# Masked neighbour maximum: the second picks of two steps summed in one PSUM tile and taken once, colliding edges sent to the subset words, seven fetches for each block

## What is computed

```python
h = jnp.maximum(_layernorm(x, axis=-1), 0.0)
x = x + max_over_neighbours(h, adj)        # jnp.max(where(adj != 0, h, -inf)) for each node
h = jnp.maximum(_layernorm(x, axis=-1), 0.0)
hw = h @ W
e = (hw @ a1)[:, None] + (hw @ a2)[None, :]
e = jnp.where(e > 0, e, 0.2 * e)
e = jnp.where(adj > 0, e, -9e15)
x = x + jax.nn.elu(jax.nn.softmax(e, axis=1) @ hw)
```

## Time and profile before

| | |
|---|---|
| median of 3 timed runs | 742.74 us (741.84 to 743.23) |
| span of the profiled execution | 753.0 us |
| busy in it: PE, DVE, ACT, POOL | 681.6, 693.7, 473.1, 281.8 us |
| TensorE's mean granted clock | 0.990 of full speed |

### The profile page before, as it was taken

One profiled execution on the slowest core, in us unless ns is written; L12 is line 12 of the kernel. 1 busy time (PEld: TensorE's weight loads), 2 busy tenths in 40 slices (PEclk: granted clock), 3 DMA queues, 4 the chain that ended last, 5 costly groups with the idle time before them and its releaser, 6 DMA issues.

```text
span 753.0 us, 14749 instructions
## 1 busy us (share of the span) xinstructions
PE 681.6 (91%) x5560; PEld 490.6 (65%) x5560; DVE 693.7 (92%) x1023; ACT 473.1 (63%) x685; POOL 281.8 (37%) x259
## 2 busy tenths in 40 slices
PE   1788999999999999999999998699999999999994
PEld 1344655555555555555555554498998999999994
DVE  8999999999999999999999999988998999889893
ACT  3888999889898899998999897562433111001000
POOL 0612034434434535444444355441620294134040
PEclk9999999999999999999999999799999999999998
DMA  9999978997888888888888746342531544443400
GB/s 305 310 355 390 344 230 270 303 327 239 268 249 247 273 258 237 272 265 241 261 263 265 246 143 228 103 143 71 187 130 62 219 140 158 156 177 130 165 15 17
DMA packets 63000, 163.07 MB, mean 217 GB/s; under 512 B 6416, under 2 KB 11152, under 8 KB 58832
## 3 DMA queue, kind: packets, MB, share of 16 engines
q1 hardware_dynamic: 53776, 138.75, 54.2%
q0 software_dynamic: 9152, 23.34, 12.1%
HBM read 117.51 MB, written 44.56 MB: 215 GB/s over the span
## 4 chain that ended last, share of the span: by engine, by line
PE 53%; DVE 31%; issue 12%; ACT 2%; DMA 1%; DVEq 0%; another core or an unknown queue 0%; SPq 0%
PE pick_ps L714 23%; DVE acc L867 20%; PE pick_ps L613 17%; DVE rest L1054 5%; PE late_ps L627 4%; PE late_ps L585 4%; PE order_ps L594 2%; PE late_ps L693 1%; PE late_ps L623 1%; DMA best<-x 1%; DVE left L889 1%; ACT depth L403 1%; DVE found L915 1%; PE late_ps L714 1%; PE order_ps L680 1%
## 5 line engine op out<-in xcount | busy, mean ns | idle before, releaser
L867 DVE TENSOR_TENSOR acc<-pick_ps,acc 128x1024 f32<-128x1024 f32 x248 | 302.6, 1220 | 20.9 <-PE pick_ps L613 12.6
L363 POOL DMA_INDIRECT found<-subset_max,tops x192 | 204.4, 1065 | 271.8 <-DVE acc L867 187.5
L1054 DVE SCALAR_TENSOR_TENSOR rest<-depth,curves_sb,stage 128x512 f32<-128x512 f32 x256 | 199.5, 821 | 15.3 <-PE pick_ps L714 3.1
L714 PE MATMUL pick_ps<-keys,rest 128*128 128x129 f32 x1792 | 207.7, 276 | 3.3 <-DVE rest L1054 3.2
L714 PEld LDWEIGHTS pick_ps<-keys,rest 128*128 128x128 f32 x1792 | 204.6, 193 | 7.4 <-DVE rest L1054 5.8
L402 ACT ACTIVATE first<-order_ps 128x1024 f16<-128x1024 f32 x128 | 131.9, 1030 | 39.1 <-PE order_ps L594 33.0
L403 ACT ACTIVATE depth<-order_ps 128x1024 f16<-128x1024 f32 x128 | 131.5, 1027 | 0.0
L613 PE MATMUL pick_ps<-first,h_hi 128*128 128x512 f16 x256 | 97.3, 380 | 17.6 <-DVE acc L867 17.1
L613 PE MATMUL pick_ps<-second,h_hi 128*128 128x512 f16 x256 | 97.2, 380 | 15.2 <-DVE acc L867 14.7
L585 PEld LDWEIGHTS late_ps<-ident_h,stage 128*128 128x128 f16 x1024 | 68.4, 99 | 50.0 <-DMA stage<-adj 12.9
L613 PE MATMUL pick_ps<-first,h_lo 128*128 128x512 f16 x256 | 97.4, 380 | 0.0
(11 more groups left out here) (146 smaller groups left out, 599.9 us busy)
## 6 DMA issues: line engine op xcount, KB each, us to landing
stage<-adj SPq DMA_DIRECT2D x64, 1024.0 KB
edge_units<-edge_t SPq DMA_DIRECT2D x64, 512.0 KB
stage<-edge_units SPq DMA_DIRECT2D x32, 1024.0 KB, 4.8
subset_max<-keys POOLq DMA_DIRECT2D x13, 512.0 KB, 9.0
found<-subset_max,tops POOLq DMA_INDIRECT x192
best<-x SPq DMA_DIRECT2D x4, 512.0 KB, 5.9
subset_max<-x POOLq DMA_DIRECT2D x4, 512.0 KB, 6.6
out<-keys POOLq DMA_DIRECT2D x7, 256.0 KB, 2.8
```

What stands on the lines that cost most here:

```text
L363: nc.gpsimd.indirect_dma_start(found[:, n % NG, s, :], None, subset_max, bass.IndirectOffsetOnAxis(tops[:, n, s:s + 1], 0)).then_inc(gathe ...
L714: last = nc.tensor.matmul(out_ps(q, b), weight[:, n % WEIGHTS, b * P:(b + 1) * P], wh[:, c, :], start=c == 0 and starts(q, b), stop=c == C ...
L867: V.tensor_tensor(acc[:, q % 2, :], pick_ps[k][:, :], acc[:, q % 2, :], ALU.max).then_inc(raised, 1)
L1054: V.scalar_tensor_tensor(out=weight[:, n % WEIGHTS, :], in0=limit[:, q % 4, :], scalar=slope[:, c:c + 1], in1=units[:, m % EDGES, k * TI:( ...
```

## The change

For an even step g and the odd step g + 1, the two `pick(., 1)` now add into one PSUM tile (start at the even step, stop at the odd one), and VectorE takes the sum once, in the odd step. A sum of two is only right if no target has a second edge in both steps in the same half. So before ScalarE makes `depth` of an odd step, TensorE adds 0.5 to every rank of a target that had a second edge in the even step (`cross`: 2 matmuls of 512 columns, of a constant tile `cross_w` with `second` of the even step, into `order_ps`). Its depth then falls between the marks: the edge is no second edge there, and `rest` (its bound moved from 1.5 to 1.25, and steeper for the sigmoid) sends it to the words. There are then more words, and 7 rows are fetched in place of 6.

`second` is made for one step at a time (128 x 1024) in place of two (128 x 2048), right behind `take(g, 0)` and two steps ahead of its use. On ScalarE `select` is split: `firsts(g + 3)`, then `later`, then `depths(g + 3)`, which in odd steps waits for `crossed`. The fetches wait for `picked` in place of `raised`, whose count is now 3 for two steps.

```diff
-SHARP = 64.0
+SHARP = 128.0
 SLOTS = 8
-FETCHES = 6
+FETCHES = 7
...
+        cross_w = sb("cross_w", [P, P], F16)
...
+        def firsts_taken(g):
+            return 3 * (g // 2) + 1 + g % 2
+
+        def seconds_taken(g):
+            return 3 * (g // 2) + 3
+
+        def fetched(n, t):
+            return 16 * ((FETCHES + 1 - t % 2) // 2 * (n // NG) + t // 2 + 1)
...
-                            pool.wait_ge(raised, 2 * (STEPS + 2 + QUAD * n) + 4 + s)
+                            pool.wait_ge(picked, 2 * (STEPS + 2 + QUAD * n) + 4 + s)
...
-                def select(g):
+                def firsts(g):
                     act.wait_ge(ordered, g + 1)
                     if g >= 4:
                         act.wait_ge(picked, 2 * g - 7)
-                        act.wait_ge(second_ready, g // 2 - 1)
+                    nc.scalar.activation(first[:, g % 4, :], order_ps[:, :], ACT.Relu, scale=-1.0, bias=1.0 - MARK).then_inc(first_ready, 1)
+
+                def depths(g):
+                    if g % 2:
+                        act.wait_ge(crossed, g // 2 + 1)
+                    if g >= 4:
+                        act.wait_ge(second_ready, g - 3)
                         if (g // 2) % 2 == 0:
                             act.wait_ge(rest_even, g // 4)
                         else:
                             act.wait_ge(rest_odd, 2 * (g // 4) - 1 + g % 2)
-                    nc.scalar.activation(first[:, g % 4, :], order_ps[:, :], ACT.Relu, scale=-1.0, bias=1.0 - MARK).then_inc(first_ready, 1)
                     nc.scalar.activation(depth[:, g % 4, :], order_ps[:, :], ACT.Abs, bias=MARK - MID).then_inc(depth_ready, 1)
...
-                select(0)
+                firsts(0)
+                depths(0)
                 high(1)
                 edges(2)
-                select(1)
+                firsts(1)
                 edges(3)
-                select(2)
+                depths(1)
+                firsts(2)
+                depths(2)
...
-                        select(g + 3)
+                        firsts(g + 3)
                     if g % 4 == 0:
                         later(g + 2)
                     elif g % 4 == 2:
                         later(g + 1)
+                    if g + 3 < PAIRS:
+                        depths(g + 3)
...
+                def cross(g):
+                    pe.wait_ge(first_ready, g + 1)
+                    pe.wait_ge(second_ready, g)
+                    for c in range(PAIR):
+                        last = nc.tensor.matmul(order_ps[:, c * TI:(c + 1) * TI], cross_w[:, :], second[:, (g - 1) % 4, c * TI:(c + 1) * TI],
+                                                start=False, stop=True, skip_group_check=True)
+                    last.then_inc(crossed, 1)
...
-                        pe.wait_ge(second_ready, g // 2 + 1)
-                    if g >= 1:
-                        pe.wait_ge(raised, 2 * (g - 1) + k + 1)
+                        pe.wait_ge(second_ready, g + 1)
+                    if k == 0 and g >= 1:
+                        pe.wait_ge(raised, firsts_taken(g - 1))
+                    elif k == 1 and g >= 2 and g % 2 == 0:
+                        pe.wait_ge(raised, seconds_taken(g - 1))
                     s = first[:, g % 4, :] if k == 0 else second[:, g % 4, :]
                     for c in range(PAIR):
                         for part, half_h in enumerate((h_hi, h_lo)):
                             last = nc.tensor.matmul(pick_ps[k][:, c * TI:(c + 1) * TI], half_h[:, p * PAIR + c, :],
-                                                    s[:, c * TI:(c + 1) * TI], start=part == 0, stop=part == 1)
+                                                    s[:, c * TI:(c + 1) * TI], start=part == 0 and (k == 0 or g % 2 == 0), stop=part == 1 and (k == 0 or g % 2 == 1))
                     last.then_inc(picked, 1)
...
                flip(3)
+                cross(1)
                 rank(2)
...
+                    if g % 2 == 0 and g + 3 < PAIRS:
+                        cross(g + 3)
...
-                def seconds(m):
-                    at = 2 * m % 4
-                    dve.wait_ge(depth_ready, 2 * m + 2)
-                    if m >= 2:
-                        dve.wait_ge(picked, 4 * (m - 1))
-                    V.tensor_scalar(second[:, at:at + 2, :], depth[:, at:at + 2, :], MID - 1, None, ALU.is_equal).then_inc(second_ready, 1)
+                def seconds(g):
+                    dve.wait_ge(depth_ready, g + 1)
+                    if g >= 4:
+                        dve.wait_ge(picked, 2 * (g - 4) + 2)
+                    V.tensor_scalar(second[:, g % 4, :], depth[:, g % 4, :], MID - 1, None, ALU.is_equal).then_inc(second_ready, 1)
...
-                        V.tensor_tensor(found[:, at, 0:3, :], found[:, at, 0:3, :], found[:, at, 3:6, :], ALU.max).then_inc(halved, 1)
+                            for t in (FETCHES - 2, FETCHES - 1):
+                                dve.wait_ge(gathered[b % NG][t % 2], fetched(b, t))
+                        V.tensor_tensor(found[:, at, 0:3, :], found[:, at, 0:3, :], found[:, at, 4:7, :], ALU.max).then_inc(halved, 1)
...
-                        V.tensor_tensor(found[:, at, 0, :], found[:, at, 0, :], found[:, at, 1, :], ALU.max).then_inc(halved, 1)
+                        V.tensor_tensor(found[:, at, 0:2, :], found[:, at, 0:2, :], found[:, at, 2:4, :], ALU.max).then_inc(halved, 1)
...
                            V.tensor_tensor(h_lo[:, 0:QUARTER, :], hs[:, 0:QUARTER, :], h_hi[:, 0:QUARTER, :], ALU.subtract).then_inc(lo_first, 1)
+                            seconds(0)
...
+                V.memset(cross_w[:, :], 0.5)
...
-                seconds(0)
+                seconds(1)
                 for g in range(PAIRS):
                     q, p = g // STEPS, g % STEPS
                     take(g, 0)
+                    if g + 2 < PAIRS:
+                        seconds(g + 2)
                     if g % 4 == 0:
                         rests(g // 2)
-                    elif g % 2 and g + 1 < PAIRS:
-                        seconds(g // 2 + 1)
                     if g == PAIRS - 2:
                         scales(0)
                     if g == PAIRS - 1:
                         stat(1)
                         moments(1)
-                    take(g, 1)
+                    if g % 2:
+                        take(g, 1)
                     if g < len(CHAINS):
```

More of the change, by code:

```diff
@@ L410, in later @@
                         act.wait_ge(digested, 2 * (m - RESTS // 2 + 1))
-                    nc.scalar.activation(rest[:, to, :], depth[:, g % 4, :], ACT.Sigmoid, scale=-SHARP, bias=SHARP * (MID - 1.5)).then_inc(rest_odd, 1)
+                    nc.scalar.activation(rest[:, to, :], depth[:, g % 4, :], ACT.Sigmoid, scale=-SHARP, bias=SHARP * (MID - 1.25)).then_inc(rest_odd, 1)
                 def key(n):
@@ L668, in sources @@
                     if q == 0:
-                        pe.wait_ge(raised, 2 * PAIRS)
+                        pe.wait_ge(raised, seconds_taken(PAIRS - 1))
                     elif q == 1:
@@ L855, in rests @@
                         dve.wait_ge(digested, 2 * (m - RESTS // 2 + 1))
-                    V.tensor_scalar(rest[:, to:to + 2, :], depth[:, at:at + 2, :], MID - 1.5, float(GROUPS), ALU.is_lt, ALU.add).then_inc(rest_even, 1)
+                    V.tensor_scalar(rest[:, to:to + 2, :], depth[:, at:at + 2, :], MID - 1.25, float(GROUPS), ALU.is_lt, ALU.add).then_inc(rest_even, 1)
                 def take(g, k):
@@ L880, in halve_two @@
                         for b in (n, n + 1):
-                            for k in range(2):
-                                dve.wait_ge(gathered[b % NG][k], 16 * FETCHES // 2 * (b // NG + 1))
-                        V.tensor_tensor(found[:, at, 0:3, :], found[:, at, 0:3, :], found[:, at, 3:6, :], ALU.max).then_inc(halved, 1)
+                            for t in (FETCHES - 2, FETCHES - 1):
+                                dve.wait_ge(gathered[b % NG][t % 2], fetched(b, t))
+                        V.tensor_tensor(found[:, at, 0:3, :], found[:, at, 0:3, :], found[:, at, 4:7, :], ALU.max).then_inc(halved, 1)
                     elif i == 1:
                         dve.wait_ge(halved, n + 1)
-                        V.tensor_tensor(found[:, at, 0, :], found[:, at, 0, :], found[:, at, 1, :], ALU.max).then_inc(halved, 1)
+                        V.tensor_tensor(found[:, at, 0:2, :], found[:, at, 0:2, :], found[:, at, 2:4, :], ALU.max).then_inc(halved, 1)
                     else:
                         dve.wait_ge(halved, n + 2)
-                        V.tensor_tensor(left[:, n:n + 2, :], found[:, at, 0, :], found[:, at, 2, :], ALU.max).then_inc(reduced, 2)
+                        V.tensor_tensor(left[:, n:n + 2, :], found[:, at, 0, :], found[:, at, 1, :], ALU.max).then_inc(reduced, 2)
                 def halve(n, i):
-                    low, high = ((0, 3), (3, 6)) if i == 0 else ((0, 1), (1, 2)) if i == 1 else ((0, 1), (2, 3))
```

(5 more changed lines are left out.)

10 lines of the change are left out of this document (5 added, 5 removed).

## The result

The changed kernel takes **755.8 us** (median of 4 runs, 754.4 to 756.2) where before takes 742.5: a ratio of 1.017 [1.0158, 1.0182]. It is slower by 13 us; 738.0 was forecast, with 729 to 750 as the range.

A forecast was written before the change was run, and what follows sets the result against it. VectorE was taken as the bound, TensorE and ScalarE close behind. Terms 1.7 - 2.4 + 1.8 - 3.8 - 0.4 - 2.4 + 0.8 = -4.7 us against the median 742.74 gave 738 us, range 729 to 750.

The forecast's parts named there:

- 3.471 us a step: Layer 0's 94 steady steps before the change, read from loads of adj in the first profile, with VectorE as bound.
- Saved: 0.04 x 94 = -3.8: Layer 0's 94 steady steps: 3.43 us a step after the change in place of 3.471, saving 3.8 us.
- The schedule of the changed kernel: Steady steps followed on TensorE: 6.73 us a pair, 6.88 with the extra digest matmul; 3.40 a step, 3.43 with late signals.
- The prediction's own sum for VectorE: VectorE's operations over eight steady steps before the change: 27.0 us, 3.37 a step; the rest was put down to waits.
- its neighbour for the ten steps behind it: Ten similar steps behind the load at 428.73 us: -0.4 us.
- The cross as the new bound: Rival, chance 0.27: TensorE's stops at the cross slow every pair, from 0.14 us a pair above the schedule; 744 to 755.
- The start: First steps: the third rank moves from 23.75 to 26.1 us behind the first cross and `depth`; +1.7 us.
- Steps 2 to 12: Steps with the chain, VectorE full: 3.68 us a step in place of 3.94, -2.4 us over nine steps.
- Steps 12 to 20: Eight steps with neither chain nor searches, already TensorE's: 3.40 us a step in place of 3.175, +1.8 us.
- The end: Two takes less where VectorE leads, -2.4; six wider layer 1 reductions, +0.8; seventh fetch hidden unless fetches land late.
- falls from first to last: VectorE in layer 0 drops to 2.80 us a step, 73 us of its work and surcharges gone, so TensorE decides.
- Nothing: Rival, chance 0.17: the cross's 0.215 us a step uses up TensorE's 0.22 of room, cancelling VectorE's gain; 742.7 us.

The follow-up runs named there:

- before again: The unchanged kernel profiled a second time: 742.66 us, ratio 0.9999, span 740.0 us.
- one pair in two: The changed kernel with sum and cross only in every second pair from step 14, plain pairs with `depth` behind `first`: 733.2 us, 0.9871.
- mixture of three: The changed kernel with sum and cross in one pair out of three from step 14, other pairs plain with `depth` behind `first`: 746.5 us, 1.0033.
- mixture of four: The changed kernel with sum and cross in one pair out of four from step 14, other pairs plain with `depth` behind `first`: 737.2 us, 0.9925.

## Why the prediction was wrong

**The step that failed** is the first one, "3.471 us a step" in what bounds the kernel now, and with it the term "Saved: 0.04 x 94 = -3.8". The schedule of the changed kernel was right (3.43; measured 3.435). What it was compared with was one execution, whose span of 753.0 stood 10 us above its timed runs, and the excess was carried over as if it lay evenly on both kernels. It lay in the very stretch that was priced: 94 x (3.471 - 3.346) = 11.8 us. The prediction's own sum for VectorE, 3.37 a step, was close to the ordinary 3.346; the difference to 3.471 was put down to waits for picks, which ordinary executions don't have. The steady term is 12.1 of the 18.6 us by which the sum misses the traces (-4.7 for 13.9).

With 3.346 and the schedule's 3.43 the term is +7.9, its neighbour for the ten steps behind it +0.8, the whole sum +8.2, and the forecast 751: slower, by the rival "The cross as the new bound". For that it needed no late signals and no `second` as long as the wide one, its "0.14 us a pair above my schedule": the schedule alone was beyond the point.

That 3.43 was met so closely is in part luck. The forecast added 0.03 a step to its 3.40 for signals that come late, and the changed kernel has none: between 100 and 420 us no take in it begins more than 0.5 us behind the last matmul of the pick it waited for. What filled the place is 0.02 a step for the wider reduction ahead of `second`, which the sum had as VectorE's time (+0.25) and not as a delay of the cross.

The other terms, by stretch:
- *The start*, +1.7: +1.9. The third rank is at 26.48 (26.1 forecast), behind the cross (24.27) and `depth` (25.32). Without the cross the 8th load comes at 38.00 us, in before again at 37.93: with the takes summed, the cross is what costs it.

The rows of it:

```profile
24.27 1.01 PE L622 MATMUL order_ps<-second,cross_w 128*128 128x512 f16 x2 [0.98 <-DVE second L882]
25.32 1.02 ACT L418 ACTIVATE depth<-order_ps 128x1024 f16<-128x1024 f32 x1 [1.39 <-PE order_ps L622]
...
26.48 1.01 PE L614 MATMUL order_ps<-edge_t,order_w 128*128 128x512 f16 x2 [1.21 <-ACT depth L418]
```

- *Steps 2 to 12*, -2.4: +0.3. The cross waits for `second` there, as the schedule had it, 4.2 us in all. Without the cross the stretch lasts 36.4 us, with it 39.98: the cross takes 3.6 us. The schedule's 7.35 us a pair is nearly met by the last two pairs (7.54 and 7.43); the longest, 9.25, holds the wait of 2.7 for the table's transfer, which no term had. The queues were not in the way of that pace on the whole: without the cross the stretch ran at 3.64 us a step with 382 GB/s.
- *Steps 12 to 20*, +1.8: +1.9.
- *The end*, -2.4 + 0.8 - 0.4: +1.4. The takes left out there were no gain that shows, and seven fetches in place of six are 1.2 us of it; the rest was not separated.
- *The mechanism*: VectorE "falls from first to last", TensorE sets the pace, two gaps in a pair of 0.15 and 0.07: measured 0.16 and 0.05. The rival "Nothing" had nearly the right arithmetic for the cross's time: 23.1 us of matmuls against 26.7 saved in layer 0, 22.8 over the whole. What it left out is the cross's waits and order, 0.22 us a pair in the steady stretch.

## What to carry to other kernels

Before costing a change against a stretch of a trace, hold the profiled execution's span against the timed runs: where it is longer by more than the effect looked for, the excess can lie all in one place (here 11.8 of 13.0 us in the 94 steps), and a stretch's own sum (here VectorE's 3.37 against 3.471 read) can tell whether it lies there. When a change trades one engine's time for another's and both are nearly full (300.5 and 307.8 of 314.6 us here), try it on a part of the steps: here one pair in two gave 9.6 us where all pairs cost 13. A delay of the cross, on the path rank, `first`, cross, `depth`, rank, was paid in full in the pair (0.15 us in every fourth); filling ScalarE's half of it with `rest` kept the price at 0.05, and the same order without the cross cost 25.8 us.

## What was not expected of the hardware

Layer 1, which is the same in all these kernels but for the seventh fetch, took 265.4 to 267.5 us from its first operation that writes `rest` to the end in eight of them (before again and the changed kernel among them), and 269.7 to 271.7 in the other five (the three without the cross's wait, and the mixtures of three and four). All those five, and no other, have one wait in it; VectorE and TensorE in the mixture of three:

```profile
551.43 1.02 DVE L938 TENSOR_TENSOR found<-found 128x384 f32<-128x384 f32 x2 [2.52 <-DMA found<-subset_max,tops]
```
```profile
555.01 1.35 PE L749 MATMUL pick_ps<-keys,rest 128*128 128x129 f32 x8 [2.41 <-DVE rest L1095]
```

and the ten us around it, there and in before again:

```profile
550.00:560.00 10.00, 6.85 (x45) 6.36 (x44) 8.01 (x25) 2.26 (x5) 0.00 (x0) 0.79 0.13 40
```
```profile
550.00:560.00 10.00, 8.92 (x77) 8.53 (x77) 9.51 (x27) 3.52 (x8) 0.00 (x0) 1.00 0.35 126
```

VectorE waits 2.5 us for the landing of a fetch, TensorE stands 2.4 us behind it, and its granted clock has a mean of 0.79 in those ten us: between its two levels, 2.4 and 1.2 GHz (1.00 and 0.5), so part of them at the lower one. The lower clock is not in all five: in the mixture of four, whose VectorE waits until 544.13 us, 540 to 550 us have 1.00. So the fetches are hidden in the changed kernel's layer 1 and not in these five, which lose 2 to 6 us by it. It is not a matter of reaching layer 1 earlier: one pair in two begins its layer 1 at 466.0 us, one in three at 473.2, and only the second has the wait. What decides it is open.

The signals of TensorE that came 1.2 us late, and with them waits for picks in ordinary steps, were seen in one execution of before alone; between 100 and 420 us no take in the other 13 traces begins more than 0.5 us behind the last matmul of the pick it waited for. What they were is open.
